# Experts layer: each block's results scattered to their tokens' rows, expert numbers packed into words, and four turned-row buffers

## The chip, the cores and the metric

One core of a Trainium2 chip runs the whole program. The metric is the device time of one execution in microseconds; the kernel before has a median of 2945.8 us in 3 runs (2944.82 to 2948.53).

The engines: TensorE (PE; its weight loads are listed as PEld), VectorE (DVE), ScalarE (ACT), GpSimd (POOL) and SyncE (SP). SP and POOL issue the DMAs of this kernel, and each engine executes its own program in order: an instruction that waits for a semaphore holds all that stands behind it on its engine.

## The reference, cut to what matters

The program is a two-layer decoder over 8 sequences of 256 tokens of width 512, so T = 2048 tokens. All of the change but a few lines lies in its last stage, a mixture of 8 experts with the two best chosen for each token, and the layer normalisation behind it:

```
scores = sigmoid(xt @ gate.T)
_, sel = top_k(scores + expert_bias, 2)
order = argsort(sel.reshape(-1), stable=True)
routed = xt[order // 2] * top_scores.reshape(-1)[order][:, None]      # to bfloat16
for e in range(8):
    h = silu(routed @ w1[e].T) * (routed @ w3[e].T)
    out_r += where(expert_ids == e, h @ w2[e].T, 0)
out = (silu(xt @ s1.T) * (xt @ s3.T)) @ s2.T
out = out.at[order // 2].add(out_r)                                   # then x + out, normalised
```

## The kernel before, in words

The function `experts` (L2706) works on eight batches n of 256 tokens (B = 8; a batch is TB = 2 tiles of 128) and then on 23 blocks j of 256 rows (BLOCKS), each block with rows of one expert only. Eight regions of 2048 rows in the DRAM tensor `rows_in` hold the rows of the eight experts; a ninth is spare.

**Routing, batches 0 to 7.** PE turns a batch (`turn_input`, L2896), ACT copies it out (`front`, L3038), PE computes the logits (`route`), DVE picks two experts (`choose`) and computes in `put` (L3133) the row of `rows_in` for each of a token's two copies; for the ranks `put` needs a product that PE makes in `count_earlier` (L2915). ACT scales the two copies by their weights (`scale`, L3051), and POOL scatters them with four indirect DMAs per batch (L2870), two copies times two tiles. PE also does the first half of the shared expert for the batch (`expand_shared`, L2933). The order on each engine is written out by hand.

**The plan.** After batch 7 DVE computes in `plan` (L3151) a table with the first row (`table[:, 0]`) and the expert (`table[:, 1]`) of each block, then `result_place`, the row of a token's result among the blocks' results. PE reads 23 expert numbers into registers, two after each product of `expand_shared(7)` (`choose_experts`, L2925). SP waits until all scatters have landed before it loads the first block.

**The blocks.** SP loads block j's rows turned, by a transposing DMA into one of three buffers `rowT` (`load_rows`, L2838). Its order is: load block j + 3, wait for the results of block j (`oe_ready`), store them to the DRAM tensor `rows_out` (L2853), next j. PE does `expand(j)` (16 products at L125, through the helper `to_features`) and then `contract(j - 1)` (4 products, L2967) into `y_psum`; between the two ACT applies silu and DVE multiplies. `take(j)` (L3191) copies `y_psum` to one of three `oe` buffers as bfloat16. POOL has nothing to do in this stage.

**The sums.** PE sums each batch into one of four pairs of PSUM banks (PAIRS = 4): `add_shared(n)` (L2971) adds x and the shared expert's second half, `add_results(n)` (L2988) the two results of each token. The order is `add_shared` 0 to 3, then `add_results(n)` for each n, each from n = 1 on followed by `add_shared(n + 3)`, which waits for the normalised batch n - 1. POOL gathers the results with four indirect DMAs per batch (`gather`, L2876), in the order gather(0), gather(1), inverse_root(0), gather(2), inverse_root(1) and so on; `inverse_root` (L77) is the reciprocal root that DVE waits for in `normal(n)` (L3197). SP stores the normalised batches.

The first stage, `self_attention`, uses idle time of POOL to fill `rows_in` with zeros (L385), waited for at its end.

Of the kernel before, what the change touches and what calls it, by code (L numbers as in the profile page):

```python
# [13 lines left out]
BF16 = mybir.dt.bfloat16  # L14
# [222 lines left out]
def self_attention(nc, A, x_in, x_out, hold):  # L237
# [3 lines left out]
    with Phase(nc, "sa", "left") as p:  # L241
# [63 lines left out]
        zeros = p.sb("zeros", [P, 4096], BF16)  # L305
        oT_psum = p.ps("oT_psum", [P, S])
# [68 lines left out]
        @block.gpsimd  # L375
        def _(g):
            g.memset(ln.minus_half[:, :], -0.5).then_inc(ln.half_set, 1)
            g.memset(zeros[:, :], 0.0).then_inc(zeros_set, 1)
            g.wait_ge(ln.half_set, ONE + 1)
            g.wait_ge(zeros_set, ONE + 1)  # L380
            chunks = hold.rows_in.rearrange("(p r) d -> p (r d)", p=P).rearrange("p (c n) -> p c n", n=zeros.shape[-1])
            for n in range(B - 1):
                inverse_root(g, ln, n)
                for c in range(3 * n, min(3 * n + 3, chunks.shape[1])):
                    g.dma_start(chunks[:, c, :], zeros[:, :]).then_inc(hold.zeroed, 16)  # L385
            g.wait_ge(hold.zeroed, 16 * chunks.shape[1])
# [2319 lines left out]
def experts(nc, A, x_in, x_out, rows_in):  # L2706
# [11 lines left out]
    PAIRS = 4  # L2718
    I32 = mybir.dt.int32
    U32 = mybir.dt.uint32  # L2720
    with Phase(nc, "ex", "right") as p:
# [19 lines left out]
        count_ps = p.sem("count_ps"); tab_ready = p.sem("tab_ready"); result_placed = p.sem("result_placed")  # L2741
        row_loaded = [p.sem(f"row_loaded{i}") for i in range(3)]
        up_ps = p.sem("up_ps"); act_ready = p.sem("act_ready"); hid_ready = p.sem("hid_ready"); down = p.sem("down")
        oe_ready = p.sem("oe_ready"); oe_stored = [p.sem(f"oe_stored{i}") for i in range(3)]
        got = [p.sem(f"got{i}", start=0) for i in range(PAIRS)]
# [45 lines left out]
        shift = p.sb("shift", [P, E])  # L2791
        moved = p.sb("moved", [P, B * 2 * TB, E])
        result_place_f = p.sb("result_place_f", [P, B * 2 * TB])
        result_place = p.sb("result_place", [P, B, 2, TB], U32)
# [6 lines left out]
        table = p.sb("table", [P, 2, BLOCKS], I32)  # L2801
# [4 lines left out]
        rowT = [p.sb(f"rowT{i}", [P, KD, S], BF16) for i in range(3)]  # L2806
# [3 lines left out]
        result = [flat(t[:, :, :]).bitcast(BF16).rearrange("p (i t d) -> p i t d", i=2, t=TB) for t in x]  # L2810
        result += [t[:, :, :, :] for t in xs] + [p.sb("result7", [P, 2, TB, D], BF16)[:, :, :, :]]
# [5 lines left out]
        logits, ranks, counts = y_psum[:, 0, 0:TB * E], y_psum[:, 1, 0:TB * E], y_psum[:, 0, 0:E]  # L2817
        sums = [[y_psum[:, 0, :], y_psum[:, 1, :]]] + [[flat(u[i][:, :, :]) for i in (0, 1)] for u in (up1, up3)]
        sums.append([bank[:, :] for bank in xin])
        rows_out = nc.dram_tensor("ex_rows_out", [BLOCKS * S, D], BF16, kind="Internal").ap()  # L2820
# [6 lines left out]
        def _(sp):  # L2827
# [33 lines left out]
        def _(g):  # L2861
            behind.late_pool(g)
            g.memset(ln.minus_half[:, :], -0.5).then_inc(ln.half_set, 1)
            g.wait_ge(ln.half_set, ONE + 1)
            for n in range(B):
# [6 lines left out]
            g.wait_ge(result_placed, ONE + 1)  # L2872
            for i in range(3):
                g.wait_ge(oe_stored[i], ONE + 16 * ((BLOCKS - 1 - i) // 3 + 1))

            def gather(n):  # L2876
                if n >= PAIRS:
                    g.wait_ge(y_ps, ONE + n - PAIRS + 1)
                for i in (0, 1):
                    for t in range(TB):  # L2880
                        g.indirect_dma_start(result[n][:, i, t, :], None, rows_out,  # L2881
                                             bass.IndirectOffsetOnAxis(ap=result_place[:, n, i, t:t + 1], axis=0))\
                            .then_inc(got[n % PAIRS], 16)

            gather(0)
            for n in range(B):
                if n + 1 < B:
                    gather(n + 1)
# [4 lines left out]
        def _(pe):  # L2893
# [21 lines left out]
            def count_earlier(n):  # L2915

                pe.wait_ge(chosen, ONE + n + 1)
                pe.wait_ge(placed, ONE + n)
                for t in range(TB):
                    out = ranks[:, t * E:(t + 1) * E]  # L2920
# [4 lines left out]
            def choose_experts(found):  # L2925

                if not found:
                    pe.wait_ge(tab_ready, ONE + 1)
                if len(found) < BLOCKS:
                    at = table[0:1, 1, len(found):len(found) + 1]  # L2930
                    found.append(pe.value_load(at, min_val=0, max_val=E - 1))

            def expand_shared(n, between=lambda found: None):  # L2933

                found = []
                if n >= 2:
                    pe.wait_ge(hid_ready, ONE + n - 1)
                for dst, w in ((up1[n % 2], s1), (up3[n % 2], s3)):
                    for m in range(KH):
                        for c in range(KD):  # L2940
                            ins = pe.matmul(dst[:, m, :], w[:, c, m * P:(m + 1) * P], xT[n][:, c, :],  # L2941
                                            start=(c == 0), stop=(c == KD - 1))
                            between(found)
                            between(found)
                ins.then_inc(up_ps, 1)
                return found

            def expand(j, e):

                pe.wait_ge(row_loaded[j % 3], ONE + 16 * (j // 3 + 1))  # L2950
                pe.wait_ge(hid_ready, ONE + B + j - 1)
                for dst, w in ((up1[j % 2], w1), (up3[j % 2], w3)):
                    by_expert = w[:, :, :].rearrange("p (e k) n -> p e k n", e=E)[:, bass.ds(e, 1), :, :]\
                        .rearrange("p e k n -> p (e k) n")
                    ins = to_features(pe, dst, by_expert, 0, rowT[j % 3], KH)
# [32 lines left out]
            def add_results(n):  # L2988

                pe.wait_ge(got[n % PAIRS], 16 * 2 * TB * (n // PAIRS + 1))  # L2990
                for t in range(TB):
                    for i in (0, 1):
                        ins = pe.matmul(sums[n % PAIRS][t], ident_b[:, :], result[n][:, i, t, :], start=False,
# [26 lines left out]
            e = expand_shared(B - 1, between=choose_experts)  # L3020
            pe.wait_ge(e_loaded, 48)
            for j in range(BLOCKS):
                expand(j, e[j])
                if j >= 1:
                    contract(j - 1, e[j - 1])
            contract(BLOCKS - 1, e[BLOCKS - 1])
# [8 lines left out]
        def _(act):  # L3035
# [43 lines left out]
            odds(2)  # L3079
            scale(1)  # L3080
            front(3)
# [15 lines left out]
        def _(v):  # L3097
            v.wait_ge(consts, ONE + 80)
            for j in range(BLOCKS):
                v.memset(numbers[:, j:j + 1], float(j))  # L3100
            v.memset(one[:, :], 1.0)
# [31 lines left out]
            def put(n):  # L3133
# [8 lines left out]
                chain(v.tensor_tensor(rank[:, :, :], ranks.rearrange("p (t e) -> p t e", t=TB),  # L3142
# [8 lines left out]
            def plan():  # L3151

                chain = Chain(v, chain_t, 16)
# [10 lines left out]
                v.tensor_scalar(table[:, 1, :], expert[:, :], float(E - 1), None, ALU.min)  # L3164
# [159 lines left out]
```

## Time and profile before

| | us |
|---|---|
| median of 3 runs | 2945.8 |
| profiled execution, its own time | 2947.47 |
| its span | 2945.7 |
| experts, first product to the first transposing load | 2674.30 to 2785.15 |
| first transposing load to the first block's product | 2785.15 to 2796.17 |
| 23 blocks | 2796.17 to 2871.70 |
| the sums, until the first normalisation is near | 2871.70 to 2890.83 |
| from there to the end | 2890.83 to 2945.7 |

Over the whole span PE is busy 90%, DVE 68%, ACT 50% and POOL 41%; the mean granted TensorE clock is 0.958 of full speed. The first seven stages take some nine tenths of the span, so these shares say little about the last one; it has to be read by its own windows. All times in the views are microseconds from the start of the span unless marked ns. In a timeline the bracket at the end of a row is the idle time before it on that engine, and what ended it.

### The profile page before, as it was taken

What the parts mean: (1) busy time and instruction counts of PE and PEld (TensorE: products, weight loads), DVE (VectorE), ACT (ScalarE), POOL (GpSimd) and SP (SyncE); (2) the same over time, 40 slices, a digit from 0 to 9 for tenths busy, and PEclk for the clock granted to TensorE, in tenths of its full rate; (3) what the DMA queues carried; (4) which work ended last, traced back from release to release, by engine and by line L of the source; (5) the groups of instructions that cost most, each with busy time, mean ns of one, the idle gap of its engine ahead of it and who ended that gap; (6) DMA issues with size and microseconds to landing.
All of it is one profiled execution on the core that took longest, in us unless ns stands there. A gap on an engine that the chain in (4) does not pass through costs nothing. (4 is left out here: it accounts for less than half of the span.)

```text
span 2945.7 us, 47353 instructions
## 1 busy us (share of the span) xinstructions
PE 2639.9 (90%) x16941; PEld 1760.8 (60%) x16941; DVE 1988.5 (68%) x2542; ACT 1464.4 (50%) x2868; POOL 1199.9 (41%) x1106
## 2 busy tenths in 40 slices
PE   8999899888888888886999899999997889997886
PEld 5666645534444444443999777777775555556653
DVE  4788757689999999966112079999999733333353
ACT  3444413289999998862222166666666311112410
POOL 0000025446666565542222058688888500001304
PEclk9999999989999999997999999999999999997898
DMA  2123513269888887964002221011112271111163
GB/s 97 65 77 116 201 51 100 77 133 168 170 170 163 170 172 162 191 154 159 32 29 74 100 79 45 26 55 58 51 51 94 77 129 36 43 66 58 61 151 118
DMA packets 534873, 296.52 MB, mean 101 GB/s; under 512 B 438160, under 2 KB 482192, under 8 KB 530832
## 3 DMA queue, kind: packets, MB, share of 16 engines
q1 hardware_dynamic: 518720, 260.31, 35.1%
q0 software_dynamic: 15952, 33.56, 4.0%
q8 instruction: 122, 2.00, 0.3%
q14 instruction: 79, 0.65, 0.1%
HBM read 126.43 MB, written 62.78 MB: 64 GB/s over the span
## 5 line engine op out<-in xcount | busy, mean ns | idle before, releaser
L1181 DVE TENSOR_REDUCE xh_top<-xh_seen 128x1 f32<-128x512 f32 (+1 forms) x768 | 631.3, 863 | 46.0 <-PE xh_seen L1083 32.5
L1153 ACT ACTIVATE xh_prob<-xh_sc,xh_bias,xh_scale 128x1024 int16<-128x1024 f32 (+1 forms) x512 | 609.8, 1201 | 69.5 <-PE xh_sc L1083 69.3
L2328 POOL TENSOR_TENSOR ss_state<-ss_du,ss_b_all 128x1024 f32<-128x1024 f32 x128 | 445.7, 3495 | 169.4 <-PE ss_turned L1926 97.8
L1083 PE MATMUL xh_seen<-xh_kT,xh_qT 96*128 96x512 bf16 x1024 | 354.0, 387 | 81.8 <-DVE xh_top L1181 79.8
L2376 DVE TENSOR_TENSOR_SCAN ss_state<-ss_decay,ss_state 128x1024 f32<-128x1024 f32 x128 | 387.3, 3027 | 27.3 <-ACT ss_decay L2178 27.3
L1083 PE MATMUL xh_sc<-xh_kT,xh_qT 96*128 96x512 bf16 x1024 | 309.0, 384 | 1.3 <-ACT xh_prob L1153 1.3
L1207 POOL CAST xh_probT<-xh_pairs 128x2048 int16<-128x2048 uint8 x128 | 241.8, 1889 | 11.3 <-DMA xh_pairs<-xh_prob 2.7
L1083 PEld LDWEIGHTS xh_seen<-xh_kT,xh_qT 96*128 96x128 bf16 x1024 | 89.3, 97 | 242.8 <-DVE xh_top L1181 220.4
L1933 PE MATMUL ss_bank<-ss_xc,hold_w_conv 128*128 128x256 f32 x1024 | 229.3, 379 | 0.7 <-ACT ss_xc L2190 0.7
L2178 ACT ACTIVATE ss_decay<-ss_delta,ss_a 128x255 f32<-128x255 f32 x512 | 210.7, 496 | 0.4
L1933 PEld LDWEIGHTS ss_bank<-ss_xc,hold_w_conv 128*128 128x128 f32 x1024 | 190.0, 189 | 26.4 <-ACT ss_xc L2190 1.1
L1107 PEld LDWEIGHTS xh_o<-xh_v_head,xh_probT 128*128 128x128 f16 x4096 | 134.9, 96 | 82.9 <-POOL xh_probT L1207 36.8
L1221 POOL TENSOR_SCALAR xh_low<-xh_top 128x1 f32<-128x1 f32 x256 | 92.3, 360 | 212.1 <-DVE xh_top L1181 211.8
L2387 DVE SCALAR_TENSOR_TENSOR ss_acc<-ss_turned,ss_c_t,ss_acc 128x512 f32<-128x512 f32 x256 | 176.3, 728 | 1.1 <-PE ss_turned L1926 1.1
L1926 PE MATMUL ss_turned<-ss_ident,ss_state 128*128 128x128 f32 x1024 | 139.3, 278 | 33.8 <-DVE ss_acc L2387 32.0
L80 POOL TENSOR_TENSOR sa_rstd<-sa_shifted,sa_minus_half 128x2 f32<-128x2 f32 x8 | 5.6, 704 | 376.9 <-DVE sa_shifted L266 376.9
L1926 PEld LDWEIGHTS ss_turned<-ss_ident,ss_state 128*128 128x128 f32 x1024 | 119.5, 143 | 59.2 <-DVE ss_state L2376 28.2
L1107 PE MATMUL xh_o<-xh_v_head,xh_probT 128*128 128x32 bf16 x4096 | 142.5, 177 | 13.5 <-DVE xo_heads_out L1170 8.5
L1083 PEld LDWEIGHTS xh_sc<-xh_kT,xh_qT 96*128 96x128 bf16 x1024 | 96.4, 98 | 77.1 <-issue 4.1
L1669 DVE TENSOR_TENSOR gf_e<-gf_y_psum,gf_b 128x1024 f16<-128x1024 f32 x8 | 9.8, 1224 | 184.5 <-PE gf_y_psum L1624 184.5
L1609 PE MATMUL gf_hid_psum<-gf_xT,gf_w 128*128 128x256 f32 x1024 | 126.1, 286 | 8.8 <-POOL gf_xT L1567 8.8
L80 POOL TENSOR_TENSOR la_rstd<-la_shifted,la_minus_half 128x2 f32<-128x2 f32 x8 | 5.5, 692 | 314.9 <-DVE la_shifted L69 314.9
(392 smaller groups left out, 4886.5 us busy)
## 6 DMA issues: line engine op xcount, KB each, us to landing
ex_rows_in<-sa_zeros POOLq DMA_DIRECT2D x18, 1024.0 KB, 6.7
ss_b_all<-ss_states SPq DMA_DIRECT2D x8, 2048.0 KB, 7.2
xa_kT<-xp_kT SPq DMA_DIRECT2D x8, 768.0 KB, 5.3
xh_qT<-xa_qT SPq DMA_DIRECT2D x48, 128.0 KB, 3.2
xh_kT<-xa_kT SPq DMA_DIRECT2D x48, 128.0 KB, 3.3
ex_rows_out<-ex_oe SPq DMA_DIRECT2D x23, 256.0 KB, 2.2
sa_x<-in_x SPq DMA_DIRECT2D x8, 512.0 KB, 3.6
sa_y<-in_x SPq DMA_DIRECT2D x8, 512.0 KB, 10.9
```

Source lines behind the costliest of these rows:

```text
L1083: ins = pe.matmul(out[:, c * D:(c + 1) * D], qT[s][:, t * P:(t + 1) * P], kT[s][:, at + c * D:at + (c + 1) * D], start=True, stop=True)
L1107: ins = pe.matmul(o[:, t, :], probT[t % RING][:, b, :].bitcast(F16), v_head[s][:, b, :], start=(b == 0), stop=(b == TT - 1))
L1153: act.activation(out, scores, ACT.Exp, bias=bias[t % RING][:, :], scale=scale[s][:, t:t + 1], accum_out=total[s][:, half, t:t + 1]).then_i ...
L1181: ins = v.tensor_reduce(top[t % RING][:, k:k + 1], scores[:, 0:n], AX.X, ALU.max)\
L1207: g.tensor_copy(probT[t % RING][:, :, :].rearrange("p (b two) q -> p b two q", two=2), pairs[t % RING][:, :, :].bitcast(U8).rearrange("p b ...
L1609: ins = pe.matmul(hid_psum[m // 2 % 3][:, m % 2, :], w0[i][:, c, m * P:(m + 1) * P], xT[:, c, :], start=(c == 0 and i == 0), stop=(c == KD ...
L1926: ins = pe.transpose(turned[r][:, m * P:(m + 1) * P], state[k % RING][:, m, t * P:(t + 1) * P], ident[:, :])
L1933: ins = pe.matmul(out, w_conv[:, k, c, m * P:(m + 1) * P], xc[:, c, k:k + S], start=(k == 0 and c == 0), stop=(k == TAPS - 1 and c == KD - 1))
L2178: ins = act.activation(decay[k % RING][:, m, 1:], delta[s][:, m, 1:], ACT.Exp, scale=a[:, m, k:k + 1])
L2328: g.tensor_tensor(state[k % RING][:, :, :], du[s][:, :, :], spread(b_all[s][:, k, :], KD), ALU.mult)\
L2376: v.tensor_tensor_scan(flat(state[k % RING][:, :, :]), flat(decay[k % RING][:, :, :]), flat(state[k % RING][:, :, :]), 0.0, ALU.mult, ALU. ...
L2387: v.scalar_tensor_tensor(acc[s][:, t, :], turned[(k * TB + t) % BANKS][:, :], c_t[s][:, t, k:k + 1], acc[s][:, t, :], ALU.mult, ALU.add).t ...
```

## The change

Every row scattered to `rows_in` now has a *name*: a second DRAM tensor `names_in`, one 4-byte number per row. Four more indirect DMAs per batch scatter the names (2 * token + copy). For each block SP loads the 256 names beside the turned rows, and POOL scatters the block's results with two indirect DMAs to the rows of a DRAM tensor `results` that the names give; rows without a token get spare rows, by numbers written in the first stage. A batch's results then lie in order, and SP loads them with one plain DMA per batch, in place of the four gathers of POOL. `result_place` and what DVE computes for it go away.

The experts of eight blocks are packed into one word (three bits each); PE reads three words after `expand_shared(7)` and takes each number out by a shift and a mask. There are four `rowT` buffers. The last batch's ranks lie in another bank, so that `count_earlier(7)` doesn't wait for `placed`. On ACT `front(3)` comes ahead of `scale(1)`.

```diff
@@ self_attention, POOL
+            g.iota(unused[:, :], [[1, unused.shape[-1]]], base=2 * T, channel_multiplier=unused.shape[-1]).then_inc(zeros_set, 1)
             g.wait_ge(ln.half_set, ONE + 1)
-            g.wait_ge(zeros_set, ONE + 1)
+            g.wait_ge(zeros_set, ONE + 2)
+            g.dma_start(hold.names_in.rearrange("(p r) o -> p (r o)", p=P), unused[:, :].bitcast(hold.names_in.dtype)).then_inc(hold.zeroed, 16)
@@ experts, SP
             def load_rows(j):
-                at = sp.value_load(table[0:1, 0, j:j + 1], min_val=0, max_val=EXPERT_ROWS - S)
+                at = sp.value_load(rows_at[0:1, j:j + 1], min_val=0, max_val=EXPERT_ROWS - S)
                 if j == 0:
                     for s in (0, 1):
-                        sp.wait_ge(scattered[s], 16 * 2 * TB * B // 2)
-                if j >= 3:
-                    sp.wait_ge(up_ps, ONE + B + j - 2)
-                sp.dma_start_transpose(rowT[j % 3][:, :, :], rows_in[bass.ds(at, S), :]).then_inc(row_loaded[j % 3], 16)
-
-            for j in range(3):
+                        sp.wait_ge(scattered[s], 16 * 4 * TB * B // 2)
+                if j >= 4:
+                    sp.wait_ge(up_ps, ONE + B + j - 3)
+                sp.dma_start_transpose(rowT[j % 4][:, :, :], rows_in[bass.ds(at, S), :]).then_inc(row_loaded[j % 4], 16)
+                if j >= NAMES:
+                    sp.wait_ge(oe_sent[(j - NAMES) % 3], 16 * TB * ((j - NAMES) // 3 + 1))
+                sp.dma_start(name[j % NAMES][:, :], names_in[bass.ds(at, S), :].rearrange("(t p) o -> p (t o)", p=P),
+                             allow_slow_non_contiguous=True).then_inc(name_loaded[j % NAMES], 16)
+
+            for j in range(BLOCKS):
                 load_rows(j)
-            for j in range(BLOCKS):
-                if j + 3 < BLOCKS:
-                    load_rows(j + 3)
-                sp.wait_ge(oe_ready, ONE + j + 1)
-                sp.dma_start(block_rows(rows_out, j * S), oe[j % 3][:, :, :]).then_inc(oe_stored[j % 3], 16)
+            for i in range(3):
+                sp.wait_ge(oe_sent[i], 16 * TB * ((BLOCKS - 1 - i) // 3 + 1))
+            for n in range(B):
+                if n >= PAIRS:
+                    sp.wait_ge(y_ps, ONE + n - PAIRS + 1)
+                sp.dma_start(result[n], results[n * 2 * S:(n + 1) * 2 * S, :]
+                             .rearrange("(t p c) d -> p t (c d)", p=P, c=2)).then_inc(got[n % PAIRS], 16)
@@ experts, POOL (NAMES = 4)
                 for i in (0, 1):
                     for t in range(TB):
+                        g.indirect_dma_start(names_in, bass.IndirectOffsetOnAxis(ap=place[:, n, i, t:t + 1], axis=0),
+                                             names[:, n, i, t:t + 1], None).then_inc(scattered[n % 2], 16)
+            for j in range(BLOCKS):
+                g.wait_ge(name_loaded[j % NAMES], ONE + 16 * (j // NAMES + 1))
+                g.wait_ge(oe_ready, ONE + j + 1)
+                for t in range(TB):
+                    g.indirect_dma_start(results, bass.IndirectOffsetOnAxis(ap=name[j % NAMES][:, t:t + 1], axis=0),
+                                         oe[j % 3][:, t, :], None).then_inc(oe_sent[j % 3], 16)
             for n in range(B):
-                if n + 1 < B:
-                    gather(n + 1)
                 inverse_root(g, ln, n)
@@ experts, PE
-                pe.wait_ge(placed, ONE + n)
+                if n < B - 1:
+                    pe.wait_ge(placed, ONE + n)
+                else:
+                    pe.wait_ge(xT_sb, ONE + B)
...
+            def load_experts():
+                pe.wait_ge(tab_ready, ONE + 1)
+                return [pe.value_load(experts_at[0:1, i:i + 1], min_val=0, max_val=E ** PER_WORD - 1) for i in range(WORDS)]
+
+            def expert(j):
+                return pe.snap((words[j // PER_WORD] >> (3 * (j % PER_WORD))) & (E - 1), min_val=0, max_val=E - 1)
...
-            e = expand_shared(B - 1, between=choose_experts)
+            expand_shared(B - 1)
+            words = load_experts()
@@ experts, ACT
-                    act.wait_ge(scattered[n % 2], 16 * 2 * TB * (n // 2))
+                    act.wait_ge(scattered[n % 2], 16 * 4 * TB * (n // 2))
...
             odds(2)
+            front(3)
             scale(1)
-            front(3)
             odds(3)
@@ experts, DVE: nine memsets at the start; in plan, before tab_ready
-                v.tensor_scalar(table[:, 1, :], expert[:, :], float(E - 1), None, ALU.min)
+                chain(v.tensor_scalar(flat(digits[:, :, :])[:, 0:BLOCKS], expert[:, :], float(E - 1), None, ALU.min))
+                chain(v.tensor_tensor(digits[:, :, :], digits[:, :, :], powers[:, :, :], ALU.mult))
+                chain(v.tensor_reduce(word[:, :], digits[:, :, :], AX.X, ALU.add))
+                chain(v.tensor_copy(experts_at[:, :], word[:, :]))
@@ experts, DVE: in take
-                    v.wait_ge(oe_stored[j % 3], ONE + 16 * (j // 3))
+                    v.wait_ge(oe_sent[j % 3], 16 * TB * (j // 3))
```

## Rows read from the trace of the kernel before

**Rows 1.** Windows: us, busy of PE, PEld, DVE, ACT, POOL; clock, DMA share, GB/s
```profile
2785.15:2796.17 11.02, 9.84 (x20) 5.46 (x21) 0.00 (x0) 0.00 (x0) 0.00 (x0) 0.56 0.35 73
2796.17:2871.70 75.53, 68.11 (x462) 44.26 (x460) 42.70 (x47) 14.33 (x24) 0.00 (x0) 1.00 0.60 147
```

**Rows 2.** Chain of waits, one turn in the block stage: start us, us, what
```profile
2834.50 3.70 DMA ex_rowT<-ex_rows_in
2838.33 2.12 PE ex_up L125 x16
2840.45 0.97 PE ex_y_psum L2967 x4
2841.42 1.75 PE ex_up L125 x16
2843.18 1.04 PE ex_y_psum L2967 x4
2844.45 1.23 DVE ex_oe L3195
2845.69 0.37 SPq L2853
2846.77 4.08 DMA ex_rowT<-ex_rows_in
```

**Rows 3.** Timeline between the last scatters and the first block
```profile
2773.73 0.97 POOL L2870 DMA_INDIRECT ex_rows_in<-ex_xs,ex_place  x1 [8.62 <-issue]
2782.60 0.96 POOL L2870 DMA_INDIRECT ex_rows_in<-ex_xs,ex_place  x1 [0.30 <-issue]
2785.15 14.52 SPq L2845 DMA_TRANSPOSE ex_rowT<-ex_rows_in  x4
2796.17 3.90 PE L125 MATMUL ex_up<-ex_rowT,ex_w 128*128 128x256 bf16 x32
```

**Rows 4.** Timeline: two points of the routing that move, and one shared expand
```profile
2702.30 2.54 ACT L3057 ACTIVATE ex_xs<-ex_x,ex_weight 128x512 bf16<-128x512 f32 x4
2705.86 3.58 PE L2911 MATMUL ex_y_psum<-ex_router,ex_xT 128*128 128x8 f32 x16 [5.25 <-ACT ex_xT L3041]
2723.13 7.15 PE L2941 MATMUL ex_up<-ex_xT,ex_s 128*128 128x256 f32 x32
2769.98 0.17 PE L2921 MATMUL ex_y_psum<-ex_both,ex_earlier 128*128 128x8 bf16 x1 [2.79 <-DVEq L3148]
```

**Rows 5.** Timeline: POOL's wake after ACT's row copies of batch 3
```profile
2733.05 2.56 ACT L3057 ACTIVATE ex_xs<-ex_x,ex_weight 128x512 bf16<-128x512 f32 x4 [0.63 <-DVEq L3148]
2736.38 0.96 POOL L2870 DMA_INDIRECT ex_rows_in<-ex_xs,ex_place  x1 [6.40 <-ACT ex_xs L3057]
```

**Rows 6.** Landing times: line 2870's scatters, then the loads of ex_rowT
```profile
DMA to landing us min/median/max: 2.4/2.4/4.4
...
DMA to landing us min/median/max: 3.0/3.3/4.9
```

**Rows 7.** Timeline: the issue of a load of 2048 single 4-byte elements
```profile
1296.81 1.58 SPq L1454 DMA_DIRECT2D gf_b<-in_L_ffn_bias  x1
```

**Rows 8.** Timeline of the sums: normalisation of batches 0 and 7
```profile
2891.73 1.30 DVE L3201 BATCH_NORM_STATS2 ex_stats<-ex_y_psum 128x6 f32<-128x512 f32 x2 [20.11 <-PE ex_y_psum L2993]
2894.36 1.53 DVE L3211 TENSOR_SCALAR ex_y_out<-ex_y_psum,ex_moments,ex_rstd 128x512 f32<-128x512 f32 x2 [0.84 <-POOL ex_rstd L80]
2934.34 1.53 DVE L3211 TENSOR_SCALAR ex_y_out<-ex_xin,ex_moments,ex_rstd 128x512 f32<-128x512 f32 x2 [0.87 <-POOL ex_rstd L80]
```

**Rows 9.** The same stretch on PE, with its waits for gathered rows
```profile
2901.83 1.03 PE L2993 MATMUL ex_up<-ex_x,ex_ident_b 128*128 128x512 bf16 x4
2907.00 1.03 PE L2993 MATMUL ex_xin<-ex_x,ex_ident_b 128*128 128x512 bf16 x4
2912.58 1.04 PE L2993 MATMUL ex_y_psum<-ex_x,ex_ident_b 128*128 128x512 bf16 x4 [0.24 <-DMA ex_x<-ex_rows_out,ex_result_place]
2929.76 1.89 PE L2993 MATMUL ex_xin<-ex_result,ex_ident_b 128*128 128x512 bf16 x4 [3.85 <-DMA ex_result<-ex_rows_out,ex_result_place]
```

More of the change, by code:

```diff
@@ L385, in _ @@
                     g.dma_start(chunks[:, c, :], zeros[:, :]).then_inc(hold.zeroed, 16)
-            g.wait_ge(hold.zeroed, 16 * chunks.shape[1])
+            g.wait_ge(hold.zeroed, 16 * (chunks.shape[1] + 1))
         @block.tensor
@@ L2718, in experts @@
     PAIRS = 4
+    NAMES = 4
+    PER_WORD = 8
+    WORDS = -(-BLOCKS // PER_WORD)
     I32 = mybir.dt.int32
@@ L2740, in experts @@
         scattered = [p.sem(f"scattered{s}", start=0) for s in (0, 1)]
-        count_ps = p.sem("count_ps"); tab_ready = p.sem("tab_ready"); result_placed = p.sem("result_placed")
-        row_loaded = [p.sem(f"row_loaded{i}") for i in range(3)]
+        count_ps = p.sem("count_ps"); tab_ready = p.sem("tab_ready")
+        row_loaded = [p.sem(f"row_loaded{i}") for i in range(4)]
         up_ps = p.sem("up_ps"); act_ready = p.sem("act_ready"); hid_ready = p.sem("hid_ready"); down = p.sem("down")
-        oe_ready = p.sem("oe_ready"); oe_stored = [p.sem(f"oe_stored{i}") for i in range(3)]
-        got = [p.sem(f"got{i}", start=0) for i in range(PAIRS)]
+        name_loaded = [p.sem(f"name_loaded{i}") for i in range(NAMES)]; named = p.sem("named")
+        oe_ready = p.sem("oe_ready"); oe_sent = [p.sem(f"oe_sent{i}", start=0) for i in range(3)]
+        got = [p.sem(f"got{i}") for i in range(PAIRS)]
         y_ps = p.sem("y_ps"); y_done = p.sem("y_done")
@@ L2790, in experts @@
         place = p.sb("place", [P, B, 2, TB], U32)
[L2791 to L2794, printed above, removed]
+        names = p.sb("names", [P, B, 2, TB], U32)
+        name = [p.sb(f"name{i}", [P, TB], U32) for i in range(NAMES)]
         blocks = p.sb("blocks", [P, E])
@@ L2805, in experts @@
         xs = [p.sb(f"xs{s}", [P, 2, TB, D], BF16) for s in (0, 1)]
-        rowT = [p.sb(f"rowT{i}", [P, KD, S], BF16) for i in range(3)]
+        rowT = [p.sb(f"rowT{i}", [P, KD, S], BF16) for i in range(4)]
         act1 = [p.sb(f"act1_{i}", [P, KH, S], BF16) for i in (0, 1)]
@@ L2923, in count_earlier, with expand_shared @@
                 ins.then_inc(cum_ps, 1)
[L2925 to L2935, printed above, removed]
+            def expand_shared(n):
                 if n >= 2:
                     pe.wait_ge(hid_ready, ONE + n - 1)
[L2938 to L2946, printed above, removed]
+                to_features(pe, up1[n % 2], s1, 0, xT[n], KH)
+                to_features(pe, up3[n % 2], s3, 0, xT[n], KH).then_inc(up_ps, 1)
+            def load_experts():
[3 more added lines that the diff above has]
+                return pe.snap((words[j // PER_WORD] >> (3 * (j % PER_WORD))) & (E - 1), min_val=0, max_val=E - 1)
             def expand(j, e):
-                pe.wait_ge(row_loaded[j % 3], ONE + 16 * (j // 3 + 1))
+                pe.wait_ge(row_loaded[j % 4], ONE + 16 * (j // 4 + 1))
                 pe.wait_ge(hid_ready, ONE + B + j - 1)
@@ L2988, in add_results @@
             def add_results(n):
-                pe.wait_ge(got[n % PAIRS], 16 * 2 * TB * (n // PAIRS + 1))
+                pe.wait_ge(got[n % PAIRS], ONE + 16 * (n // PAIRS + 1))
                 for t in range(TB):
                     for i in (0, 1):
-                        ins = pe.matmul(sums[n % PAIRS][t], ident_b[:, :], result[n][:, i, t, :], start=False,
+                        ins = pe.matmul(sums[n % PAIRS][t], ident_b[:, :], result[n][:, t, i * D:(i + 1) * D], start=False,
                                         stop=(i == 1), skip_group_check=True)
@@ L3100, in _ @@
                 v.memset(numbers[:, j:j + 1], float(j))
+            v.memset(digits[:, :, :], 0.0)
+            for i in range(PER_WORD):
+                v.memset(powers[:, :, i:i + 1], float(E ** i))
             v.memset(one[:, :], 1.0)
@@ L3141, in put @@
                 v.wait_ge(cum_ps, ONE + n + 1)
-                chain(v.tensor_tensor(rank[:, :, :], ranks.rearrange("p (t e) -> p t e", t=TB),
+                chain(v.tensor_tensor(rank[:, :, :], ranks[n == B - 1].rearrange("p (t e) -> p t e", t=TB),
                                       spread(base[:, :], TB), ALU.add))
@@ L3151, in plan @@
             def plan():
-                chain = Chain(v, chain_t, 16)
+                chain = Chain(v, chain_t, 15)
                 v.wait_ge(count_ps, ONE + 1)
@@ L3258, in decoder @@
               state_space(nc, A, after[2], after[3], hold), linear_attention(nc, A, after[3], after[4], hold),
-              experts(nc, A, after[4], out, hold.rows_in)]
+              experts(nc, A, after[4], out, hold.rows_in, hold.names_in)]
     phases = [next(stages[0])]
```

56 lines of the change are left out of this document (25 added, 31 removed).

## The prediction

> **What bounds the kernel now.** The change lies in the last 270 us but for a few lines, so I read the windows of that stretch first, then the chain of waits, then the timeline where the chain turns.
>
> In the block stage PE is busy 68.1 of 75.53 us at full clock, yet 23 blocks in 75.53 us are 3.28 us a block, and 16 + 4 products need about 2.8 us [rows 1]. The chain shows the rest: the load of a turned block lands (3.70), PE works through expand, contract, expand, contract (2.12 + 0.97 + 1.75 + 1.04), DVE copies the result (1.23), SP issues the store (0.37) and the register read behind it, and only then the transposing load of the block four further on starts. From load to load that is 2834.50 to 2846.77 = 12.27 us for four blocks, 3.1 a block [rows 2]. So the loop is bound by the delay from a block's result to a later block's rows, not by PE. The reader is to see that the load stands behind the store on SP: 2846.77 - 2845.69 = 1.08 us from store to load.
>
> In front of the blocks PE is held by its own register reads: 20 products took 9.84 us, 0.49 each, at a granted clock of 0.56, close to the 1.2 GHz level of its two [rows 1], where 32 of them took 7.15, 0.22 each, without reads [rows 4]. Behind the blocks POOL's gathers set the pace.
>
> **The start of the blocks.** Removed: 23 register reads among the products. PE starts `expand_shared(6)` 2.79 us sooner, since the last ranks wait for nothing [rows 4], and with the swap below it starts both at 2764.8; 64 products of 0.22 end near 2779. But the turned rows now come later. POOL issues one indirect DMA per 1.26 us (0.96 + 0.30) [rows 3]; a batch has eight in place of four. From batch 3 (2736.38 [rows 5]) to batch 6 (2773.73) a batch comes every 12.5 us, and 8 x 1.26 = 10.1, so the names of the earlier batches hide. Batches 6 and 7 come together: before, eight issues ran from 2773.73 to 2782.60 and the load of block 0 began 2.55 us after the last [rows 3]. Now there are sixteen. The swap on ACT lets PE have batch 3 sooner by most of the 2.54 us of the copies it passes, for PE stood idle 5.25 us there and the chain runs through it [rows 4]; I take 2.35, a little under the 2.54, for the exponential that still goes first. `scale(1)` is later by some 1.1 us, for which nothing waits: POOL begins with batch 0 as ACT turns to batch 1 (2702.30) and has ten microseconds of work. So batch 6 starts scattering at 2771.4, the last issue starts at 2771.4 + 15 x 1.26 = 2790.3, block 0's load at 2792.9: 7.7 us later than before. It lands after 3.3 [rows 6], at 2796.2, just when the first block began before (2796.17): the register reads had cost PE what the names now cost POOL. But PE has been idle for some 16 us by then. Its clock was down to 0.56 after mere gaps, so I let the first expand run at the lower level: 3.7 us for 1.9. It ends at 2800.1, the second at 2802.9. Before, the first two took 3.90 together and ended at 2800.1 [rows 3]. Net: +2.8 us.
>
> A scatter of names I take at the 1.26 of a row scatter, for the count of indices is the same (128), a 256th of the bytes or not; the bounds 0.96 (no gap between issues) and 1.6 are -2.4 to +2.7 us for the eight that count.
>
> **The block loop.** SP's order is now: load block j, wait until the results of block j - 4 have landed in `results`, load the names of j, next j. So the load of block k + 5 stands behind the scatter of block k, where before the load of block k + 4 stood behind the issue of its store. Queued behind this wait: name load, register read and the next transposing load, and PE waits for that.
>
> From the end of expand(j): contract(j - 1) and the copy end 2.5 us later (1.04 + 0.23 + 1.23) [rows 2]; POOL wakes in 0.77 us (ACT ends at 2735.61, POOL starts at 2736.38 [rows 5]); the second scatter starts 1.26 later and lands after 2.4 [rows 6]; SP issues the name load and the next transposing load 1.1 us after [rows 2] (the name load taken at the price of the store); that lands after 3.7 (the row of the chain; median 3.3, longest 4.9) [rows 2, 6]; PE starts 0.13 later and takes 2.1. Sum: 2.5 + 0.8 + 1.26 + 2.4 + 1.1 + 3.7 + 0.13 + 2.1 = 14.0 us for four blocks, 3.5 a block against 3.1. The fourth buffer gives one block more of slack, 3.1 us; waiting for the scatter to land in place of issuing a store takes away 0.8 + 1.26 + 2.4 = 4.5.
>
> Blocks 0 to 4 find their rows there. The turn starts at the end of block 1's expand (2802.9); blocks 5, 9, 13, 17, 21 end 14.0 apart, the last at 2872.9; block 22 some 2.8 later, 2875.7. Before, its expand ended at 2866.6 and the sums began 5.1 later (2871.7). So the sums begin at 2880.8: +9.1 us, the 2.8 of the start within.
>
> Bounds for the terms that no row shows: POOL's wake 0.1 to 1.4; a scatter's landing while transposing loads run 2.1 to 4.4 (2.4 was measured in a quiet stretch, the longest is 4.4 [rows 6]); the name load's issue 0.4 to 0.65. The nearest row for the last is a load of 2048 single 4-byte elements: 1.58 us to issue [rows 7]; 256 of them, an eighth, should be near the 0.37 of the store, so I take that. Turn: 12.6 to 17, times five: -7 to +15 us around the value.
>
> The Trainium skill, "DMA: Bandwidth & Descriptors" (Specifications), says that transfers under 512 B make the DMA engine read, modify and write, which speaks against names of 4 bytes. No row of before shows a 4-byte write, so the trace can't agree or disagree; were it to double the landing of the name scatters from 2.4 to 4.8, the start would move by 2.4 us and the loop not at all, as names are read there and not written.
>
> At nothing: the shift and mask per block (PE's sequencer does them while it waits for rows; without that cover 23 x 2 x 0.13 = 6 us, an estimate: (0.49 - 0.22) / 2 for one read of before); three chained DVE operations more ahead of `tab_ready`, 0.6 us, with 16 us to spare before block 0's load; nine memsets on DVE at the start, ahead of a wait for PE; the fill of the names in the first stage, where POOL has nothing to do; `take` waiting for scatter j - 3, landed 2 us before.
>
> **The sums.** From 2871.7 to 2890.8 PE adds the shared part of four batches, as before; the last scatter and SP's loads (under 9 us) hide there. Then before: POOL does four gathers (5.0 us) between two inverse roots, and batches come 5.75 us apart; PE waits 3.85 us for the last [rows 9]. Without gathers two things remain. DVE needs 2891.73 to 2895.89 = 4.16 us a batch, the root within [rows 8]. PE needs 5.17 for `add_shared` and `add_results` together (2901.83 to 2907.00), as long as there is a batch to add. In the times of before: batch 3 starts on PE at 2907.00 [rows 9], batch 4 at 2912.2 (2912.58 before), batch 5 at 2917.4; DVE takes batch 5 from 2918.4 (PE's 1.04 later), and three batches of 4.16 end at 2930.9. Before, the last ended at 2934.34 + 1.53 = 2935.9 [rows 8]. Gain 5.0 us; bounds 4 (PE's clock falls again after its wait for batch 0) to 8 (PE faster too). The store's landing behind it is unchanged.
>
> **Sum.** +2.8 (start) + 6.3 (loop) - 5.0 (sums) = +4.1 us. The profiled execution took 2947.47 for a span of 2945.7, so the next would have a span of 2949.8 and 2951.6; the median of the runs lies 1.7 under the profiled one, so 2945.8 + 4.1 = 2949.9.
>
> **Rivals.**
> - *The wait for the scatter is longer under load* (slower). Place: SP's wait for `oe_sent`. The block stage moves 147 GB/s with DMA engines 60% busy [rows 1]; a scatter that lands after 4.4 there in place of 2.4 [rows 6] makes a turn 16.0, five turns +10, the total +14: 2960. It decides from a landing of about 2.8 on, where the total passes 5.9. Against it: stores and loads of the same stretch landed within their usual times. The Trainium skill ("DMA: Bandwidth & Descriptors", Latency and other measured facts) gives an HBM access 0.2 us on average and 2 us at high load; by the second figure the same +10 would come out.
> - *The names hold nobody up, and the fourth buffer pays* (faster). If POOL wakes at once, the scatter lands in 2.1 and the transposing loads, without 256 KB of stores on their queue, land in 3.0, the turn is 2.5 + 0.1 + 1.26 + 2.1 + 1.1 + 3.0 + 0.13 + 2.1 = 12.3: five turns -8.5 against my value, total -4.4: 2941.4; with PE warm at the first block -1.8 more, 2939.6. For it: before, the median load landed in 3.3 and only the late ones bound. Against it: POOL's wake was 0.77 or more wherever I looked.
> - *The start is what goes wrong*: the 2.35 us of the swap are not kept, or a name scatter costs POOL more than a row scatter: total +5 to +8, 2952.5.
> - *The gain in the sums doesn't come*, as the result loads of 512 KB are late or PE's clock is low: total +9, 2955.
>
> **Numbers.** Forecast as worked out 48%, with a range of its own of 2945 to 2955; longer under load 20%; faster 15%; the start 10%; the sums 7%. A change within 0.2% (5.9 us) is about what a measurement of this kernel can't tell from none. Of the forecast's share 38 points lie within 0.2%, 8 above, 2 below; the rival under load gives 20 slower; the fast one 11 faster and 4 the same; the start 5 slower and 5 the same; the sums 7 slower. Faster 13, same 47, slower 40. Range 2941 to 2960: the lower end is the fast rival's, the upper that of the wait under load.
>
> **What would show it.** Block 0's transposing load near 2793, the first block's products near 2796.3 at the lower clock level; in the chain of the block stage DVE `ex_oe`, POOL's scatter to `ex_results`, its landing, then SP's name load and the load of `ex_rowT`, with 14 us for four blocks; no wait of PE for gathered rows at the end, and batches 4.2 to 5.2 us apart. The forecast is wrong if blocks take 3.1 us or less each, if PE's clock doesn't fall before block 0, or if the last batches still come 5.7 apart.

## The result, and the profile after

The changed kernel takes 2989.15 us (median of 4 runs, 2983.49 to 2994.2) against 2946.91 for the kernel before: a ratio of 1.0143, 95% interval 1.0121 to 1.0165. It is slower by 42 us. The forecast was 2949.9 with a range up to 2960, so it was wrong, and not by a little.

The profiled execution took 2994.2 us for a span of 2992.4. I cut the last stage of every profile at the same four points: PE's first transposing of the stage, the issue of block 0's load, PE's first product of block 0, and PE's first product of the sums with the shared expert's weights. (The last point lies 0.9 us behind the transposing products at which the windows of the views end.) In us:

```
                        stage start   to load 0   to block 0   blocks   sums to end
before                     2674.3       110.8        11.1        76.4       73.1
predicted                  2674.3       118.6         3.3        85.5       68.1
after                      2678.6       133.3         4.0        95.7       80.8
names 64 B apart (e1)      2672.4       117.6         3.4        99.0       80.1
load order (e3)            2670.8       132.4         4.2        96.8       73.1
eight name buffers (e4)    2671.1       132.7         4.0        73.0       83.0
the three together (e5)    2673.4       117.6         3.6        70.5       71.6
before + words (e6)        2670.7       110.8         3.7        78.7       73.0
before + 4 rowT (e7)       2679.8       111.8        11.0        67.4       71.8
name in the row (e8)       2679.7       109.4         3.5        72.8       69.1
before + both (e9)         2676.8       110.9         3.6        68.3       71.6
plain loads (e12)          2676.6       111.8        10.9        77.0       65.5
```

The stage's start differs by up to 10 us between executions of stages that the change hardly touches, so single profiles are compared by their segments and kernels by their ratios. Three of the four segments came out longer than predicted: 15 us in the routing, 10 in the blocks, 13 in the sums.

The windows of after that answer to [rows 1]; columns are us, busy of PE, PEld, DVE, ACT and POOL, the granted clock, DMA share, GB/s:

```profile
2811.93:2815.94 4.01, 0.00 (x0) 0.01 (x1) 0.00 (x0) 0.00 (x0) 0.00 (x0) 0.50 0.47 66
2815.94:2910.71 94.77, 73.71 (x452) 49.03 (x460) 42.21 (x46) 13.73 (x23) 41.81 (x44) 0.88 0.55 122
2910.71:2992.40 81.69, 46.82 (x158) 23.92 (x160) 25.57 (x56) 0.00 (x0) 7.83 (x11) 0.79 0.30 108
```

In the block stage PE stands still for 21 us in place of 7, POOL has 42 us of work where it had none, and the granted clock is 0.88 where it was 1.00. In front of block 0 it is 0.50, the 1.2 GHz level.

**The routing.** The chain of waits (start us, us, what) where it leaves the pattern of before, ACT's first row copy behind that wait, and the landing times of the name scatters and then of the row scatters, which landed in 2.4 to 4.4 before [rows 6]:

```profile
2713.99 0.96 POOL ex_names_in L2894
2714.95 0.30 issue
2715.25 21.06 DMA ex_names_in<-ex_names,ex_place
...
2804.61 7.16 DMA ex_names_in<-ex_names,ex_place
2811.93 3.72 DMA ex_rowT<-ex_rows_in
...
2815.94 6.36 PE ex_up L125 x32
```
```profile
2736.39 2.56 ACT L3069 ACTIVATE ex_xs<-ex_x,ex_weight 128x512 bf16<-128x512 f32 x4 [13.69 <-DMA ex_names_in<-ex_names,ex_place]
```
```profile
DMA to landing us min/median/max: 2.1/6.7/21.1
DMA to landing us min/median/max: 2.4/5.8/19.0
```

A scatter of names takes POOL 0.96 + 0.30, as taken. But the fourth one of batch 0 lands 21 us after its issue, ACT waits for that before it may overwrite its row copies, and PE waits for ACT. The last one before block 0 takes 7.16, where I had 2.6 from last issue to load. In the same trace's packets, 27 of the 1024 packets of row scatters took over 1 us, up to 14.0 (the median is 0.18), 20 of them in one stretch of some 8 us; in before none took over 0.51.

**The blocks.** One turn of the chain, to be laid beside [rows 2]:

```profile
2863.30 4.31 DMA ex_rowT<-ex_rows_in
2867.61 0.32 issue
2867.94 2.74 PE ex_up L125 x16
2870.90 1.50 PE ex_y_psum L2975 x3
2872.42 1.24 DVE ex_oe L3204
2873.70 0.70 issue
2874.41 0.96 POOL ex_results L2900
2875.36 0.30 issue
2875.67 2.40 DMA ex_results<-ex_oe,ex_name
2878.20 0.39 SPq L2860
2878.64 0.28 SPq L2851
2879.30 3.41 DMA ex_rowT<-ex_rows_in
```

The mechanism is the predicted one, step for step: copy, POOL's wake (0.70), second scatter after 1.26, its landing (2.40), name load, next transposing load. But a turn of four blocks is 16.0 us, not 14.0; the others measure 16.5, 16.3 and 15.4 (the transposing loads of blocks 5, 9, 13, 17 and 21 start at 2830.49, 2847.01, 2863.30, 2879.30 and 2894.70). SP's waits in the stage, and the load of block 21 and the slowest expand behind such a wait:

```profile
SPq L2860 <- DMA ex_results<-ex_oe,ex_name: 26.7, 11, 5.5
```
```profile
2894.70 1.25 SPq L2857 DMA_TRANSPOSE ex_rowT<-ex_rows_in  x1
2883.04 3.51 PE L125 MATMUL ex_up<-ex_rowT,ex_w 128*128 128x256 bf16 x16 [2.34 <-DMA ex_rowT<-ex_rows_in]
```

**The sums.** Who waited for whom from 2910 on (in total, times, longest), and the chain where it turns:

```profile
DVE ex_y_out L3220 <- DMA out<-ex_y_out: 8.9, 1, 8.9
...
PE ex_up L2990 <- DVE ex_y_out L3220: 7.1, 1, 7.1
```
```profile
2945.79 0.88 PE ex_xin L3001 x4
2946.68 0.36 SPq L2870
2947.09 5.08 DMA out<-ex_y_out
2952.20 1.54 DVE ex_y_out L3220 x2
```

PE's sum of batch 3 (L3001) releases SP's result load of batch 7, and only behind that does SP issue the first store of the stage, 12.4 us after batch 0 was ready (DVE ended it at 2934.66). `y_out` has two buffers, so DVE stands until that store has landed.

### The profile page after: what moved, and what is told of

Read it like the earlier page. It is cut to its first block and busy times, and to the rows that moved or that the text cites. A ratio compares the mean times of both kernels' runs of the same rounds, so it can differ in the third digit from the quotient of the medians.

```text
span 2992.4 us, 47464 instructions
## 1 busy us (share of the span) xinstructions
PE 2641.8 (88%) x16931; PEld 1765.5 (59%) x16941; DVE 1988.1 (66%) x2548; ACT 1464.5 (49%) x2868; POOL 1241.0 (41%) x1155
```

## Experiments

All ratios are against the kernel before on the same chip, with 95% intervals.

**The scatters of names.** e1 puts each name at the head of a 64-byte piece, e2 at the head of one of 512 bytes; a write stays 4 bytes.

```diff
-    names_in [EXPERT_ROWS, 1];   index place
+    names_in [EXPERT_ROWS, 16];  index name_at = 16 * place     (e2: 128)
```

> One name per 64 bytes of DRAM in place of one per 4; the scatter still writes 4 bytes per row (one DVE operation more per batch for the index times 16, and the first fill is 16 times as large). Theory A (names of one expert are neighbours, so the scatter's writes fall into the same piece of DRAM and wait for each other): names land after 2.5 to 3 us in place of 6.6, ACT no longer waits 13.7 and 6.5 us for them, the blocks start 20 us sooner, time near 2967. Theory B (any write of 4 bytes is slow, wherever it goes): landing stays at 6 to 7, time 2985 to 2994. Theory C (eight indirect DMAs per batch are too many for POOL's queue): as B.

> The same with one name per 512 bytes. Theory A with a piece of 64 bytes: as the run with 64. Theory A with a larger piece (up to 512): names land after about 2.5 us only here, and only partly sooner with 64. Theory B and C: landing stays at 6 to 7 us in both.

e1: 2972.59, 1.0091 (1.0074 to 1.0107). e2: 2973.25, 1.0103 (1.0082 to 1.0125). Block 0's load comes 117.6 us after the stage's start in both. The scatters land in 1.7/2.1/7.1 us (min, median, max), no row packet took over 0.44, and ACT's wait for names shrinks from 20.2 us to 0.6. The last name scatter in front of block 0 lands in 2.13 in place of 7.16:

```profile
2787.68 2.13 DMA ex_names_in<-ex_names,ex_name_at
```

So a 4-byte write is not slow in itself; it was something about 4-byte writes side by side. (The blocks of e1 take 99.0 in place of 95.7, which no run explains.)

e10 and e11 put names 16 and 32 bytes apart, to see how wide the piece is.

```diff
+    names_in [EXPERT_ROWS, 4];   index name_at = 4 * place      (e11: 8)
```

> The changed kernel with names 16 bytes apart (64 apart in the first experiment). Theory A (what slows the writes is how many names fall into one 64-byte piece of memory): with four in a piece in place of sixteen the scatters of names still land late, 3 us or more in the median and 10 or more at the longest, and block 0's load comes between 118 and 133 us after the stage's start. Theory B (only writes that touch the same or the next 4 to 8 bytes hinder one another): landing median 2.1 and longest 7.2 as at 64 bytes, load at 117.6 us, 2972.

> The changed kernel with names 32 bytes apart. Theory A (a piece of 64 bytes is what writes share): two names in a piece, landing a little above that at 64 bytes apart, load of block 0 at 118 to 122 us. If the piece is 32 bytes, landing and load are as at 64 bytes (2.1 median, 7.1 longest; 117.6 us), and only the 16-byte kernel is late.

e10: 2992.3, 1.016 (1.0138 to 1.0183). e11: 2997.83, 1.0177 (1.0154 to 1.02); loads at 138.6 and 137.7 us. By the times alone Theory A would stand. The traces say otherwise: in neither did a packet of the row scatters take over 0.44 us, at 16 bytes as little as at 32. In their place ACT stands still with its input ready. PE's next product after the shared expand starts at 2713.82, and ACT takes the expand at 2722.53, 8.7 us later. The timeline of ACT in e11 (remote: the view finds no instruction or DMA that released it):

```profile
2705.14 1.28 ACT L3082 ACT_TABLE_LOAD   x1
2722.53 0.60 ACT L3082 ACTIVATE ex_shared<-ex_up 128x512 f32<-128x512 f32 x1 [16.10 <-remote]
```

These 8.7 us are less than half of the 20 by which the load is late. The rest builds up in the batches behind them and isn't taken apart: PE's next routing products take 3.58 us where e15 has 1.95, and ACT stands for another 3.6 us at 2756.

One more thing differed from e1: there the fill of `names_in` in the first stage was two transfers with a wait behind each, here one. And the group ran on another chip. e13 to e16, all on one chip, take up spacing and fill.

```diff
e13  the changed kernel as it is
e14  e1 as it was
e15  e11, filled by two transfers with a wait behind each in place of one
e16  e13, filled by two transfers with a wait behind each in place of one
```

> The changed kernel itself, once more, as the control of this group (same chip as the next three). Load of block 0 at 133 us after the stage's start and 2983 to 2994 if the late start belongs to the program; if it belongs to the chip, another time here.

> The kernel of the first experiment (names 64 bytes apart, written in the first stage by two fills with a wait behind each) once more on this chip. Load at 117.6 us and 2972 if the spacing is what mended it there; if the chip was, as late as the 16- and 32-byte kernels (138 us, 2990).

> Names 32 bytes apart as in the last group, but filled by two transfers with a wait behind each, as the 64-byte kernel does and the 32-byte kernel did not. Theory (the spacing counts): load at 138 us, 2990 to 3000, as with one fill. Rival (not the spacing but the fill, the only other thing in which the good and the bad kernels differ): 117.6 us, 2972.

> The changed kernel with names at neighbouring words as they are, filled in two transfers with a wait behind each. Theory (spacing): load at 133 us or later, 2983 to 2994. Rival (fill): 117.6 us, 2972.

```
                                      us        ratio (interval)           load 0
e13  4 B apart,  one fill           2990.7    1.0149 (1.012 to 1.0178)     132.0
e16  4 B apart,  two fills          2985.26   1.0128 (1.0111 to 1.0145)    135.2
e15  32 B apart, two fills          2973.41   1.0097 (1.008 to 1.0113)     117.6
e14  64 B apart, two fills          2973.54   1.0091 (1.0065 to 1.0118)    117.6
e11  32 B apart, one fill (other chip)  2997.83   1.0177 (1.0154 to 1.02)  137.7
```

The changed kernel and e1 repeat on this chip (e13, e14). Spacing is settled: on one chip and with the same fill, e16 against e15, 4 bytes apart is 17.6 us late and 32 bytes apart is not; in ACT's waits on names, e16 and then e15:

```profile
ACT ex_xs L3073 <- DMA ex_names_in<-ex_names,ex_place: 18.5, 2, 14.3
```
```profile
ACT ex_xs L3074 <- DMA ex_names_in<-ex_names,ex_name_at: 0.7, 1, 0.7
```

The burst of slow packets (23 to 27 of 1024 over 1 us) is in all five profiles with names at neighbouring words (after, e3, e4, e13, e16) and in none of the others. Theory A's 64-byte piece fell: 32 bytes are enough. By the packets of e10 16 bytes are enough too, but its time can't confirm that. The delay of e10 and e11 is another one, and e15 doesn't have it. ACT's row of e15 at that point:

```profile
2713.14 0.60 ACT L3082 ACTIVATE ex_shared<-ex_up 128x512 f32<-128x512 f32 x1 [7.65 <-PE ex_up L125]
```

What holds ACT in e10 and e11 is open. e11 and e15 differ in the fill (one transfer or two, and the size of its buffer), 2.7 ms earlier, but also in the chip, and no kernel with two fills ran on the chip of e10 and e11. Nor is a single fill enough by itself: the changed kernel and e13 have one too (with no wait of its own behind it), and there ACT took the same expand as soon as it ended.

**The order of SP in the sums.** e3:

```diff
-            for n in range(B): load result n
-            for n in range(B): store n
+            for n in range(PAIRS): load result n
+            for n in range(B): load result n + PAIRS; store n
```

> SP issues result loads 0 to 3, then load n + 4 and the store of batch n in turn, in place of all eight loads ahead of all stores. Theory: the sums lose 5 to 8 us since the first stores stand behind load 7, which waits for batch 3; then no 8.9 us wait of DVE for a store, time 8 us less, 2981. Rival (the sums are longer because PE's clock is low): less than 2 us gained.

2976.95, 1.0105 (1.0088 to 1.0122). The sums take 73.1 in place of 80.8, and DVE's wait for a store is gone.

**The names' buffers.** e4 has eight in place of four, so SP's wait is for the results of block j - 8.

```diff
-    NAMES = 4
+    NAMES = 8
```

> Eight name buffers in place of four, so a turned block's load no longer stands behind the scatter of the block before it. Theory: the chain of scatter landing, name load, turned load goes away; a block takes 2.9 to 3.1 us in place of 4.1, the expands at the lower clock go away too, time 15 to 25 us less, 2967. Rival (the transposing loads themselves, beside scatters, are the bound): under 5 us less.

2962.71, 1.0058 (1.0042 to 1.0075), the largest single gain: the blocks fall from 95.7 to 73.0 us, and of the scatters to `ex_results` SP waits only for the last. The window of the blocks, and SP's only wait for such a scatter:

```profile
2807.80:2880.80 73.00, 65.81 (x456) 46.71 (x465) 42.15 (x46) 13.73 (x23) 42.36 (x45) 0.94 0.75 158
```
```profile
SPq L2866 <- DMA ex_results<-ex_oe,ex_name: 17.4, 1, 17.4
```

**All three mended.** e5 is e1, e3 and e4 in one.

> The changed kernel with names 64 bytes apart, SP's order of loads and stores mended, and eight name buffers: the three causes together. Theory (these three are the whole loss): routing 117.6 us to block 0's load, 3.4 to the first product, blocks 73, sums and end 73, 267 us in all against 271.4 before, so 2941. Rival (they hide each other, or something else is left): 2950 or more.

2940.38 (10 runs), 0.9993 (0.9983 to 1.0002): 1.5% or some 44 us below the changed kernel by the two ratios, and even with the one before.

**Parts of the change alone, on the kernel before.** e6 has only the packed expert numbers, e7 only the fourth buffer of turned rows, e9 both; results are stored by block and gathered, as before.

```diff
e6   -  e = expand_shared(B - 1, between=choose_experts)
     +  expand_shared(B - 1); words = load_experts(); e = expert(j)
e7   -  rowT = [... for i in range(3)]
     +  rowT = [... for i in range(4)]
```

> The kernel before with one part of the change, the packed expert numbers (3 register reads after the last shared expand, in place of 23 among its products). Theory: the first block's product comes 4 us after block 0's load in place of 11, PE doesn't fall to the lower clock for long, the rest is unchanged: 2938 to 2940. Rival (the shift and mask per block cost PE what the reads did): within 2 us of before.

> The kernel before with one part of the change, four buffers of turned rows in place of three, loads four ahead of stores. Theory (the chain load, four PE groups, copy, store, load is bound to the number of buffers): 2.8 to 2.9 us a block in place of 3.1, blocks 68 to 70 us in place of 76: 2938 to 2940. Rival (the transposing loads, at a DMA share of 0.6 to 0.7, are the bound): no change.

> The kernel before with both parts that paid alone: the packed expert numbers and four buffers of turned rows; results still stored in block order and gathered at the end. Theory (the two gains lie in different stretches: 7.4 us of the gap in front of the blocks, 9 us of the blocks): stage start to block 0's load 111, gap 3.7, blocks 67 to 70, sums 72 to 73: about 16 us below the kernel before, 2928 to 2932, and SP's last wait at the closing barrier 5.4 us, as there are 64 indirect DMAs. Rival (the words make the blocks slower, as the run with the words alone lengthened them by 2.3 us, since PE comes to them cold): blocks 72 or more, 2935 or above.

e6: 2938.05, 0.9982 (0.9972 to 0.9992). e7: 2933.47, 0.9967 (0.9954 to 0.9979). e9: 2927.72, 0.9935 (0.9918 to 0.9952), the lowest of all. The two gains add: 7.5 us of the gap before block 0 and 8 us of the blocks (76.4 to 68.3), which e9 runs at full clock:

```profile
2791.30:2859.60 68.30, 63.70 (x457) 45.03 (x466) 42.01 (x46) 13.73 (x23) 0.00 (x0) 1.00 0.73 170
```

**The name inside the row.** e8 keeps the scatter of results, but appends the name to its token's row (1088 bytes in place of 1024), so that one scatter carries both; with e3's order and eight buffers.

```diff
-    scatter xs -> rows_in;  scatter names -> names_in
+    scatter (xs, name) -> rows_in [.., D + 32]
```

> As the run with three causes mended, but the name travels in the row itself: a row of `rows_in` is 1024 + 64 bytes, one scatter of 1088 bytes per 128 rows in place of two, and no name scatter at all; POOL writes the names into the scaled rows first (two iotas a batch). Theory (the name scatters' issue on POOL is what delays the start once their landing is mended): block 0's load 108 to 111 us after the stage's start, blocks 73, sums 73: 2931 to 2934, faster than before. Rival (PE's clock at the start and the longer end take it back): 2940.

2930.5, 0.9957 (0.9943 to 0.9971). That is faster than before, but e8 also contains the packed words and the fourth buffer, which alone give 0.9935 in e9 (the intervals overlap). So no run shows a gain from scattering the results itself.

**The end of the sums.** In e3 the sums are mended and yet no shorter than before. Its last `y_out` ends at 2963.8, 13.5 us before the end, where before that distance was 9.8. SP's wait at the closing barrier had grown. Before (64 indirect DMAs issued), e8 (78) and after (110):

```profile
SPq L3273 <- PEq L3273: 5.4, 1, 5.4
```
```profile
SPq L3285 <- PEq L3285: 6.6, 1, 6.6
```
```profile
SPq L3283 <- PEq L3283: 9.2, 1, 9.2
```

e12 tests that it goes with their number. It is the kernel before with its gathers left out (results are summed by block and not by token), plain loads in their place, 32 indirect DMAs left.

```diff
-    POOL: for n: 4 indirect gathers of results
+    SP:   for n: load n + PAIRS (2 plain loads of 256 KB); store n
```

> The kernel before with its 32 gathers left out: two plain loads of 256 KB a batch on SP's queue take their place (load n + 4 and store n in turn), so results are added in block order and not to their tokens. 32 indirect DMAs are left in place of 64. Theory (SP's wait at the closing barrier grows by 0.083 us for each indirect DMA that the kernel issued: 5.4 us for 64, 6.6 for 78, 9.2 for 110): 2.7 us here. Rival (the wait depends on something else, as on the number of semaphores or on POOL having late DMAs): 5.4 as before, or 9.2. The sums should gain about 3.7 us in the normalisations besides, to 66 us with the barrier's gain, and the time come to some 2938 to 2940.

2937.86, 0.9973 (0.996 to 0.9985). The wait is

```profile
SPq L3272 <- PEq L3272: 3.4, 1, 3.4
```

It fell, by 2.0 us and not by the 2.7 expected. Four kernels lie in order: 3.4, 5.4, 6.6, 9.2 us for 32, 64, 78, 110 of them; from pair to pair 0.06 to 0.09 us each. All kernels with 64 (e6, e7, e9) show 5.4 and all with 110 show 9.2. The number orders it; what the barrier does with them the trace doesn't show. The sums took 65.5 us: 7.6 less than before, 2.0 of it the barrier; the other 5.6 I put down to the gathers.

## Why the prediction was wrong, step by step

The cause of the loss is not the rival to which I gave the slower side. That one was a scatter landing late in the block stage: on the chain it landed in 2.39 to 2.75, below the 2.8 from which that rival would have decided (of all 46 scatters of results the median is 2.7 and the longest 6.8). A turn did take the 16 us that this rival named, but from other terms.

*Removed reads* (right). Gap 11.1 to 4.0 here, 3.7 in e6 alone.

*Names cost POOL eight issues more before block 0: +7.7* (right in itself, wrong in sum). With spaced names the load comes 6.8 us later than before. The step that failed is "the names of the earlier batches hide". I looked at POOL's issue time and gave the landing a bound of double; the landing holds ACT's row buffers (`scale(n)` waits for the scatters of n - 2), and at neighbouring words it was up to 21 us. Cost 15.7 us (133.3 against 117.6 in e1), 5.0 of it in the last landing and the rest in ACT's waits. The read-modify-write rule of the Trainium skill ("DMA: Bandwidth & Descriptors", Specifications), which I had weighed as doubling 2.4, brought no such delay by size alone: 4-byte writes 32 bytes or more apart landed in 2.1 in the median, sooner than the 1024-byte rows. A read-modify-write of one piece by several writes would fit what neighbours did, but no run shows the mechanism.

*PE cold at block 0* (right). Granted clock 0.50, the first two expands 6.36 us together; predicted 3.7 and 2.8.

*A turn of 14.0 us* (right mechanism, mis-sized, and one term missing). Measured 15.4 to 16.5. In the turn shown: POOL's wake, issue and landing 0.70 + 1.26 + 2.40 = 4.4 (predicted 0.8 + 1.26 + 2.4), name load and register read 1.2 (1.1). What was off is PE's own part, the expand behind the wait, 2.72 to 3.51 for 2.1 (15.8 us over blocks 5, 9, 13, 17 and 21 for 10.5), and the transposing load, 4.55, 4.43, 4.31 and then 3.41 for 3.7. The expands are about half of the 10 us by which the blocks exceed the forecast. The missing term is that the turn feeds on itself: PE idles while it waits for the rows, its clock over the stage is granted at 0.88, and the expand behind the wait is slow. I had counted the cold clock once, at block 0, and not in every turn. e4 shows the size of the whole: without the wait on names 22.7 us are gone and the clock is 0.94.

*The fourth buffer: one block of slack, 3.1 us* (too little by itself). Alone it is worth 9.0 us (e7), more than the 7.4 that PE idled in before's blocks would suggest for one block; in the changed kernel SP's waits in front of the name loads (26.7 us) stood in its way.

*The sums: -5.0* (failed). Without gathers the sums gained 5.6 us in e12, so that term was right. Two things that I didn't look at took it back. I followed PE, DVE and POOL through the sums and not SP's queue: eight result loads stand ahead of all stores, load 7 waits for the sum of batch 3, and the first store with it. +7.7 us (e3). And the closing barrier is 3.8 longer, which no row of before could tell. Together -5.6 + 7.7 + 3.8 = 5.9 of the 7.7 measured; the other 1.8 are open.

*The swap on ACT, 2.35 us* (right): PE's wait there fell from 5.25 us [rows 4] to 2.82.

By segments, after less before: routing +22.5 (+7.8 foreseen), gap -7.1 (-7.8), blocks +19.3 (+9.1), sums +7.7 (-5.0): +42.4 us, and the medians are 42.2 apart.

## What to carry to other kernels

When an instruction with a wait is put into a queue, walk every queue it is put in to the end and ask of each later entry what now stands behind that wait: here SP's name loads in the blocks (22.7 us) and its stores in the sums (7.7 us) were both lost so. A ring that closes through a landing needs buffers for the whole turn, and a turn in which PE idles must be priced at PE's lower clock. Keep small scattered writes 32 bytes or more apart, or carry them in a row that is scattered anyway, and take a mixed change apart: two of its parts alone gave 0.9935, the whole 1.0143.

## What the runs showed of the hardware

Scatters of single 4-byte words to neighbouring words brought on one burst in which packets of other scatters too took up to 14.0 us in place of 0.18; at 16 (e10), 32, 64 and 512 bytes apart there was none. The issue of an indirect DMA of 128 indices costs POOL 0.96 us and 0.30 to the next, for 4 bytes an index as for 1024. The wait at the closing barrier rose with the number of indirect DMAs issued, 3.4 us at 32 to 9.2 us at 110. In e10 and e11 ACT stood 8.7 us with its input ready; whether that goes with the fill of `names_in` or with the chip no run shows.
